# The opening of a hybrid block: raw rows into the projection, the root of the norm applied behind it, loads and first tables re-ordered

## The reference

```python
x = x + attn_a(ln(x))   # the "stack": Win 512 -> 64, 4 layers, Wout 64 -> 512
x = x + ffn(ln(x))      # gate, up, silu, down; weights w * (su @ sv), 512 -> 1792 -> 512
x = x + attn_b(ln(x))   # 32 heads, alibi, softmax, Wo
x = x + ffn(ln(x))      # the same weights again
# attn_a:
h = x @ Win.T + bin
for each of 4 layers:
    y = silu(layernorm(h) * ln1_w + ln1_b)
    h = h + sconv(y, phazor, last_conv) * sc_lin     # a complex linear recurrence over the sequence
    y = silu((layernorm(h) * ln2_w + ln2_b) @ W1.T + b1)
    h = h + y @ W2.T + b2
return (layernorm(h) * lnl_w + lnl_b) @ Wout.T + bout
```

## Time and profile before

| | |
|---|---|
| median of three runs | 2368.31 us |
| the profiled execution | 2372.38 us |
| its span in the trace | 2371.1 us |
| PE busy | 2328.1 us, 98% of the span |
| DVE, ACT, POOL busy | 67%, 51%, 35% |
| granted TensorE clock, mean | 0.993 of full speed |
| start of the first gate matmul | 117.28 us |

### The profile page before, as it was taken

How to read it: one execution, slowest core, us unless ns; L and a number is a source line. 1 busy time by engine, 2 the same in 40 slices (tenths; PEclk the granted TensorE clock), 3 DMA queues, 4 the chain that set the end, 5 groups by cost and what they waited for, 6 DMA issues and landing times.

```text
span 2371.1 us, 40814 instructions
## 1 busy us (share of the span) xinstructions
PE 2328.1 (98%) x12672; PEld 2015.7 (85%) x12672; DVE 1589.5 (67%) x3900; ACT 1218.3 (51%) x3827; POOL 838.5 (35%) x1332
## 2 busy tenths in 40 slices
PE   6899999999999999999999999999999999999999
PEld 4577777888899999999999999999999988888887
DVE  7666664534277777777777777777777776565553
ACT  7543332233266666666666666766766661232212
POOL 5550443212034445444454554444544440010000
PEclk8899999999999999999999999999999999999999
DMA  4335567987831534536346346364362225565554
GB/s 144 105 144 199 203 237 281 346 342 280 314 125 63 236 145 164 231 139 233 147 150 235 124 157 244 131 231 165 137 249 92 95 70 204 189 219 195 189 192 160
DMA packets 92627, 444.84 MB, mean 188 GB/s; under 512 B 10168, under 2 KB 17336, under 8 KB 72704
## 3 DMA queue, kind: packets, MB, share of 16 engines
q1 hardware_dynamic: 91056, 440.78, 50.5%
q10 hardware_dynamic: 1360, 1.46, 0.2%
HBM read 342.59 MB, written 99.61 MB: 186 GB/s over the span
## 4 chain that ended last, share of the span: by engine, by line
PE 93%; DVE 2%; DMA 1%; ACT 1%; POOL 1%; issue 1%; SPq 0%; DVEq 0%; POOLq 0%; ACTq 0%
PE psum L837 80%; PE psum L2832 4%; PE psum L2786 2%; PE psum L2821 1%; PE psum L2822 1%; PE psum L2777 1%; POOL x L1292 0%; POOL srstd L1262 0%; DMA wD<-weff_dn 0%; DMA short_raw<-in_lr_short 0%; DMA weff_s<-short_st 0%; PE psum L1812 0%; PE psum L1981 0%; PE psum L1959 0%; PE psum L1971 0%
## 5 line engine op out<-in xcount | busy, mean ns | idle before, releaser
L837 PE MATMUL psum<-qw,xs 128*128 128x384 f32 x2688 | 548.6, 346 | 0.2 <-DVE su L2630 0.2
L837 PEld LDWEIGHTS psum<-qw,xs 128*128 128x128 f32 x2688 | 457.8, 188 | 1.0 <-issue 0.4
L2603 POOL TENSOR_SCALAR prob<-prob,rsum 128x128 f32<-128x128 f32 (+1 forms) x512 | 228.9, 460 | 527.3 <-DVE rsum L2711 527.2
L2545 ACT ACTIVATE prob<-biased,nmax 128x256 f32<-128x256 f32 (+1 forms) x512 | 227.2, 446 | 151.0 <-DVE nmax L2701 147.7
L2719 DVE TENSOR_TENSOR oT_l<-psum,oT_h 128x512 fp32r<-128x512 f32 x128 | 88.5, 692 | 193.9 <-ACT oT_h L2557 193.9
L837 PE MATMUL psum<-wo_h,oT_h 128*128 128x512 f32 x512 | 208.5, 407 | 0.0
L837 PE MATMUL psum<-wo_l,oT_h 128*128 128x512 f32 x512 | 203.5, 397 | 0.0
L837 PE MATMUL psum<-wo_h,oT_l 128*128 128x512 f32 x512 | 202.0, 394 | 0.0
L2486 ACT ACTIVATE squares<-cc 128x128 f32<-128x128 f32 x512 | 154.3, 305 | 41.0 <-DVE cc L2633 31.4
L2552 ACT ACTIVATE pT_h<-psum 128x384 fp32r<-128x384 f32 x256 | 125.2, 489 | 76.1 <-PE psum L2832 73.7
L2569 POOL TENSOR_TENSOR rr<-ss,mneg_half 128x6 f32<-128x6 f32 (+1 forms) x128 | 150.1, 1173 | 10.7
(11 more groups left out here) (360 smaller groups left out, 5863.9 us busy)
## 6 DMA issues: line engine op xcount, KB each, us to landing
xs<-weff_x SPq DMA_DIRECT2D x62, 1792.0 KB, 7.9
wgu<-weff_gu SPq DMA_DIRECT2D x42, 1024.0 KB, 7.4
qw<-weff_q SPq DMA_DIRECT2D x56, 768.0 KB, 7.8
weff_q<-q_parts SPq DMA_DIRECT2D x84, 384.0 KB, 2.4
wD<-weff_dn SPq DMA_DIRECT2D x56, 512.0 KB, 4.8
wS<-weff_s SPq DMA_DIRECT2D x28, 1024.0 KB, 7.2
wdn<-weff_dn SPq DMA_DIRECT2D x42, 512.0 KB, 4.6
weff_gu<-wgu SPq DMA_DIRECT2D x14, 1024.0 KB, 4.0
```

Of the source, the lines that this page charges most:

```text
L837: ins = pe.matmul(out_ap, stat[a], mov[b], start=start and n == 0, stop=stop and n == last)
L2545: act.activation(prob[:, b, lo:hi], biased[:, b % 2, lo:hi], ACT.Exp, bias=nmax[:, b, t:t + 1], scale=-1.0, accum_out=esum[:, b, t:t + 1]) ...
L2603: pool.tensor_scalar(prob[:, b, lo:hi], prob[:, b, lo:hi], rsum[:, b, t:t + 1], 1.0, ALU.mult, ALU.mult).then_inc(prob_done, 1)
```

## The change

- **Rows.** The row step is gone. xT transposes the raw rows of x as soon as they have landed, and proj multiplies them. Win is centred over its input side too, so the mean of a row drops out: wcol (4 matmuls with a column of -0.5) gives the sums and one more DVE operation in winc subtracts them. The root of the norm is applied behind the projection: wide0 (ACT) copies the roots of four tiles out to 64 columns each, across (2 transposes) and roots (ACT copy) bring them along the columns, hs (DVE) multiplies. sq and h of norm 0 follow hs. This holds for all four stacks.
- **Odd norms of the lead.** w1 multiplies h itself, not the normed h. wc (two ACT copies of 128x512) takes the products out of PSUM; rtr makes the root for all 512 columns (four transposes), hm (two DVE products of 128x512) applies it, and hid works from SBUF. idw stands ahead of rtr. yn is gone here.
- **Norm 8, all stacks.** rtr, yn and wide are gone; out multiplies h, xadd multiplies by the root per row as it adds. The lead's second out waits for eps.
- **Products of the lead.** pr moves from DVE to POOL, pi from POOL to DVE.
- **Setting up.** root, rho, turn, tab0, scan0, winc and wcol get urgency 0. b1f now follows var 0.
- **Loads.** w1, b1, w2, wout and bout (seven DMAs, 1.3 MB) are issued by SP between the lead's rows and the rows of stack 1, instead of by ACT.
- **First gate.** Its first half takes the eight products with the high part of x and waits for fxhi alone; the second half, the four with the low part, waits for fxlo. frow 2 and 3 write into free buffers instead of the ring of two.

The diff, cut to its core (indentation shortened by eight; bookkeeping of semaphores and banks left out):

```diff
-    room = ("proj", 1, 0) if s == 3 else None
+    room = [("proj", 1, 0)] if s == 3 else []
...
-        o.add(("row", s, j), "dve" if lead else "act", 0.6, [("inv", 0, 2 * s + j // 2)] + ([("row", s, j - 1)] if j else [room] if room else []), urg,
-              ("row", 1))
-        o.add(("xT", s, j), "pe", 0.9 if lead else 0.45 * slow, [("row", s, j)] + ([("xc", s, j - 2)] if j > 1 and lead else []), urg,
-              bank, ("row", s, j))
-        step(("xc", s, j), "act", 0.6, [("xT", s, j)], ("xT", s, j))
-    pe_step(("proj", s, 0), 2.5 if lead else 1.75, [("xc", s, j) for j in range(TPB)] + [("winc", 0, 0)], bank)
+        landed = (("begin", 0, 0), 5.5 + 0.8 * j if lead else 13.0 + 3.0 * s)
+        o.add(("xT", s, j), "pe", 0.9 if lead else 0.45 * slow, [landed] + room + ([("xc", s, j - 2)] if j > 1 and lead else []) +
+              ([("xT", s, j - 1)] if j else [("xT", s - 1, TPB - 1)] if s else []), urg, bank)
+        step(("xc", s, j), "act", 0.6, [("xT", s, j)] + room, ("xT", s, j))
+    step(("wide0", s, 0), "act", 0.45, [("inv", 0, 2 * s), ("inv", 0, 2 * s + 1)])
+    pe_step(("across", s, 0), 0.25, [("wide0", s, 0), ("fold", 0, 0)], bank)
+    step(("roots", s, 0), "act", 0.4, [("across", s, 0)], ("across", s, 0))
+    pe_step(("proj", s, 0), 3.2 if lead else 1.75, [("xc", s, j) for j in range(TPB)] + [("winc", 0, 0)], bank)
+    step(("hs", s, 0), "dve", 0.43, [("proj", s, 0), ("roots", s, 0)], ("proj", s, 0))
...
-        made = ("conv", s, l) if odd else ("w2", s, l - 1) if n else ("proj", s, 0)
+        made = ("conv", s, l) if odd else ("w2", s, l - 1) if n else ("hs", s, 0)
...
-            step(("h", s, n), "dve", 0.42, [("sq", s, n)], made)
+            step(("h", s, n), "dve", 0.42, [("sq", s, n)], made if n else None)
...
+        if n == NORMS - 1:
+            break
+        if lead and odd:
+            pe_step(("w1", s, l), 1.5, [("h", s, n), ("fold", 2, l)])
+            pe_step(("idw", s, l), 0.45, [("h", s, n)])
+            step(("wc", s, l), "act", 1.3, [("w1", s, l)])
+            pe_step(("rtr", s, n), 0.45, [("rstd", s, n)])
+            step(("hm", s, l), "dve", 1.4, [("rtr", s, n), ("wc", s, l)])
+            step(("hid", s, l), "act", 1.3, [(("hm", s, l), -0.6), ("fold", 3, 0)])
+            pe_step(("w2", s, l), 0.9, [("hid", s, l), ("fold", 4, 0), ("idw", s, l)])
+            continue
...
-        if n == NORMS - 1:
-            break
...
-            step(("pi", s, l), "pool", 0.83, [("zi", s, l)])
-            step(("pr", s, l), "dve", 0.4, [("zr", s, l), ("zi", s, l)])
+            if lead:
+                step(("pr", s, l), "pool", 0.83, [("zr", s, l)])
+                step(("pi", s, l), "dve", 0.4, [("zi", s, l)])
+            else:
+                step(("pi", s, l), "pool", 0.83, [("zi", s, l)])
+                step(("pr", s, l), "dve", 0.4, [("zr", s, l), ("zi", s, l)])
...
-            if lead:
-                pe_step(("idw", s, l), 0.45, [("h", s, n)])
-            pe_step(("w2", s, l), 0.9, [("hid", s, l), ("fold", 4, 0)] + ([("idw", s, l)] if lead else []), bank)
+            pe_step(("w2", s, l), 0.9, [("hid", s, l), ("fold", 4, 0)], bank)
...
-        o.add(("bout", s, t), "pool", 1.27, [("fold", 5, 0), ("row", s, t), ("w1", 0, t) if lead else ("frow", 0, TPB - 1)], 6)
+        o.add(("bout", s, t), "pool", 1.27, [("fold", 5, 0), ("xT", s, t), ("inv", 0, 2 * s + t // 2), ("w1", 0, t) if lead else ("frow", 0, TPB - 1)], 6)
...
-        pe_step(("out", s, j), 0.95, [("yn", s, NORMS - 1), ("fold", 6, 0)], pair)
-        step(("xadd", s, j), "dve", 1.4, [("out", s, j), ("bout", s, j), ("bout", s, SJ + j)], ("out", s, j))
+        pe_step(("out", s, j), 0.95, [("h", s, NORMS - 1), ("eps" if lead else "rstd", s, NORMS - 1), ("fold", 6, 0)], pair)
+        step(("xadd", s, j), "dve", 1.4, [("out", s, j), ("rstd", s, NORMS - 1), ("bout", s, j), ("bout", s, SJ + j)],
+             ("out", s, j))
...
-    o.add(("root", 0, 0), "dve", 1.6, [("ri", 0, 0)], 1)
-    o.add(("rho", 0, 0), "act", 0.3, [("root", 0, 0)], 1)
+    o.add(("root", 0, 0), "dve", 1.6, [("ri", 0, 0)], 0)
+    o.add(("rho", 0, 0), "act", 0.3, [("root", 0, 0)], 0)
...
-        o.add(("turn", k, 0), "pool", 1.0 if k else 0.2, [("turn", k - 1, 0) if k else ("root", 0, 0)], 1)
-        o.add(("tab0", k, 0), "dve", 0.42 + 0.002 * (1 << k), [("turn", k, 0)] + ([("tab0", k - 1, 0)] if k else []), 1)
+        o.add(("turn", k, 0), "pool", 0.9 if k else 0.2, [("turn", k - 1, 0) if k else ("root", 0, 0)], 0)
+        o.add(("tab0", k, 0), "dve", 0.42 + 0.002 * (1 << k), [("turn", k, 0)] + ([("tab0", k - 1, 0)] if k else []), 0)
...
-    o.add(("winc", 0, 0), "dve", 1.0, [(began, 6.0)], 1)
-    o.add(("scan0", 0, 0), "dve", 1.2, [("root", 0, 0)], 1)
+    o.add(("wcol", 0, 0), "pe", 0.4, [(began, 4.8)], 0)
+    o.add(("winc", 0, 0), "dve", 1.6, [("wcol", 0, 0)], 0)
+    o.add(("scan0", 0, 0), "dve", 1.2, [("root", 0, 0)], 0)
...
-    o.add(("b1f", 0, 0), "pe", 3.6, [(began, 9.7)], 1, ("bank", 1, "early"))
+    o.add(("b1f", 0, 0), "pe", 2.2, [("var", 0, 0), (began, 9.7)], 1, ("bank", 1, "early"))
...
-            o.add(("gate", n, h), "pe", 1.36, here + [("fxlo", T, TPB - 1)] + ([last] if last else []) + (
+            o.add(("gate", n, h), "pe", 1.36 if n else (1.82, 0.91)[h], here + [
+                ("fxlo" if n or h else "fxhi", T, TPB - 1)] + ([last] if last else []) + (
...
+    for g in range(NG2):
+        rows = slice(g * DIM, (g + 1) * DIM)
+        sp.dma_start(w1_sb[rows, :, :], w1).then_inc(small_in, 16)
+    sp.dma_start(b1_sb[:], b1).then_inc(small_in, 16)
+    sp.dma_start(w2_c[:], w2).then_inc(w2_in, 16)
+    for g in range(NG2):
+        rows = slice(g * DIM, (g + 1) * DIM)
+        sp.dma_start(wout_sb[rows, :], wout).then_inc(wout_in, 16)
+    sp.dma_start(bout_sb[:], bout.partition_broadcast(P)).then_inc(wout_in, 16)
...
-    for g in range(NG2):
-        rows = slice(g * DIM, (g + 1) * DIM)
-        act.dma_start(w1_sb[rows, :, :], w1).then_inc(small_in, 16)
-    act.dma_start(b1_sb[:], b1).then_inc(small_in, 16)
-    act.dma_start(w2_c[:], w2).then_inc(w2_in, 16)
-    for g in range(NG2):
-        rows = slice(g * DIM, (g + 1) * DIM)
-        act.dma_start(wout_sb[rows, :], wout).then_inc(wout_in, 16)
-    act.dma_start(bout_sb[:], bout.partition_broadcast(P)).then_inc(wout_in, 16)
...
-        elif what == "row":
-            t = a * TPB + b
-            dst = wait_row(act, (what, a, b))
-            act.wait_ge(inv_done[0], 2 * a + b // 2 + 1)
-            act.activation(dst, x[:, t, :], ACT.Identity, bias=ln_nmr[:, t:t + 1],
-                           scale=ln_rstd[:, t:t + 1]).then_inc(stk_act[a], 1)
+        elif what == "wide0":
+            act.wait_ge(inv_done[0], 2 * a + 2)
+            roots = ln_rstd[:, a * TPB:(a + 1) * TPB].rearrange("p (g j o) -> p g j o", g=NG2, o=1)
+            act.activation(buf_b[q][:].rearrange("p (j g d) -> p g j d", j=SJ, g=NG2),
+                           roots.broadcast_to([P, NG2, SJ, DIM]), ACT.Copy).then_inc(stk_act[a], 1)
+        elif what == "roots":
+            act.wait_ge(stk_pe[a], ON_PE[a]["across", 0])
+            act.activation(buf_a[q][:], psum[:, stack_bank(a, "across", 0), 0:SW], ACT.Copy).then_inc(stk_act[a], 1)
...
+        elif what == "wc":
+            act.wait_ge(stk_pe[a], ON_PE[a]["w1", b])
+            bank = pair_bank(a, "w1", b)
+            for c in range(FC):
+                act.activation(hidden[:, q, c, :].rearrange("p (g t) -> p g t", g=NG2),
+                               psum[:, bank:bank + NG2, c * SW:(c + 1) * SW], ACT.Copy).then_inc(stk_act[a], 1)
...
-            act.wait_ge(stk_pe[a], ON_PE[a]["w1", b])
...
+            if lead:
+                for c in range(FC):
+                    act.wait_ge(stk_dve[a], ON_DVE[a]["hm", b, c])
+                    act.activation(hidden[:, q, c, :], hidden[:, q, c, :], ACT.Silu,
+                                   bias=b1_sb[:, b, c:c + 1]).then_inc(stk_act[a], 1)
+                continue
+            act.wait_ge(stk_pe[a], ON_PE[a]["w1", b])
...
-        elif what == "row":
-            dve_rows(wait_row(dve, (what, a, b)), 0, a * TPB + b).then_inc(stk_dve[a], 1)
+        elif what == "hs":
+            dve.wait_ge(stk_pe[a], ON_PE[a]["proj", 0])
+            dve.wait_ge(stk_act[a], ON_ACT[a]["roots", 0])
+            dve.tensor_tensor(hres[q][:], psum[:, stack_bank(a, "proj", 0), 0:SW], buf_a[q][:], ALU.mult).then_inc(stk_dve[a], 1)
...
-                ins = dve.tensor_scalar(hres[q][:], psum[:, stack_bank(a, "proj", 0), 0:SW], col_c("bin"), None, ALU.add)
+                ins = dve.tensor_scalar(hres[q][:], hres[q][:], col_c("bin"), None, ALU.add)
...
+        elif what == "pi":
+            dve.wait_ge(stk_dve[a], ON_DVE[a]["zi", b])
+            dve.tensor_tensor(buf_b[q][:], buf_a[q][:], sinT[:, b, :], ALU.mult).then_inc(stk_dve[a], 1)
+        elif what == "hm":
+            dve.wait_ge(stk_pe[a], ON_PE[a]["rtr", 2 * b + 1])
+            for c in range(FC):
```

(57 more changed lines are left out.)

72 lines of the change are left out of this document (45 added, 27 removed).

## The result

The changed kernel is slower: median 2375.78 us of 17 runs, against 2369.57 of as many runs of the kernel before; ratio 1.0023, 95% interval 1.0015 to 1.003. I had forecast 2363.1. Its profiled execution took 2377.15 us, its span is 2375.8, 4.7 above that of before.

The account below looks back on a forecast made before the run. TensorE was taken as full from 117.3 us, the lead's chain of waits as the bound before it. Terms +2.5 -0.5 -4.6 -4.0 -1.5 = -8.1, shadow +2.9, net -5.2: 2363.1 us, range 2354 to 2370.

Parts of the forecast that it names:

- Step 1: Opening up to silu: ACT stalls in lr 0 until its loads land near 20.4; +2.5 us.
- Step 2: Lead's even norms: pi on DVE ends sooner, pr on POOL hardly earlier; 0.15 us a layer, -0.5 us.
- Step 3: Lead's odd norms: shorter chain behind rtr, w1 and wc hidden; 1.15 us a layer, -4.6 us.
- Step 4: Norm 8: out no longer waits for the root, xadd applies it and ends earlier; -4.0 us.
- Step 5: First gate: starts right behind fxhi, its eight products hide fxlo, free frow buffers; -1.5 us.
- Shadow: TensorE work of other stacks that must run behind the earlier gate: 0.36 per us gained, +2.9 us.
- Sum: All five steps: -8.1 us at the first gate, near 109.2; net -5.2 us after shadow work is paid back.
- C: Opening, slower: 1.3 MB ahead in the queue delays low-rank loads to 26, lengthening ACT's stall; 2370.3 us; chance 0.1.
- B: Paid back: lead shortens, but shadow work falls behind and PE repays nearly all; -1.5, 2367 us; chance 0.2.
- A: Opening, no stall: lr 0 behind the lead's first steps or loads early; -17.6 at the gate, 2357 us; chance 0.2.
- The chance for slower: Whole kernel slower by over 0.2%: only the end of C and things not seen; chance 0.09.

Follow-up runs that it names:

- e6: Changed kernel with the eight small loads (w1, b1, w2, wout, bout) issued by ACT again, as before; median 2374.25 us.
- e1: Changed kernel with the swap undone: the lead's pr on DVE and pi on POOL again; median 2374.53 us.
- e18: Changed kernel with two planned times moved: lr 0 at 25.0, raw rows of stacks 1 to 3 at 22, 25, 28; median 2363.39 us.
- e11: Changed kernel with five spare 128x256 matmuls ahead of conv's wait for pr in each of the lead's layers 1 to 3; median 2369.40 us.
- e7: Kernel before the change with only norm 8 and the first gate changed; median 2367.77 us.
- e4: Changed kernel with five spare 128x256 matmuls ahead of the lead's wait for pr in all four layers; median 2372.45 us.
- e8: Kernel before the change with five spare 128x256 matmuls per lead layer ahead of conv's wait for pr; median 2379.45 us.
- e13: As e11, against the changed kernel, with the eight small loads also issued by ACT as before; median 2370.24 us.
- e17: e11 with lr 0 planned at 25.0 and raw rows of stacks 1 to 3 at 22, 25, 28; median 2365.48 us.
- e2: Changed kernel with one planned time moved: low-rank factors (lr 0) ready at 20.0 us instead of 12.0; median 2373.07 us.
- e16: e11 with lr 0 planned as ready at 20.0; median 2368.20 us.

## Why the prediction was wrong, step by step

**Step 1, right.** Forecast: lr 0 stalls ACT until 20.4, square at 25.4, silu at 30.7. Measured: 20.34, 25.50, 31.08; +2.9 on silu for +2.5. The order that I worked is the one that ran up to the first square. Between it and silu I was right by luck: I had two statistics there, 3.6 us, and the trace has one, with three copies of raw rows and a fold of wout in the other's place. The tables bound nothing, but they were ready at 28.33 and not near 21, because DVE stood in hs for 7.3 us and they were queued behind it. The table load was followed at once by silu, at 29.79 + 1.28 = 31.07 and 31.08, so the drain of 1380 ns of the Trainium skill (ScalarE: Activation LUTs, What ACT_TABLE_LOAD costs) is not seen here either. The first square is at 25.50 us with the loads issued by SP and at 25.44 with ACT (e6). By the rule of the Trainium skill (DMA: Bandwidth & Descriptors, Issuing engines are not separate DMA queues) moving issues saves issue time alone; this pair agrees, within the scatter of the landings given at e6.

**Step 2, near in size by luck, and blind to its effect.** The even blocks, from square to square, took 40.7 us for 41.55: -0.8 for -0.5 (-1.6 if layer 0 is counted from silu, as step 1 was). But the mechanism did not come. I had pi at 0.4 us on DVE and pr at 0.8 to 0.9 on POOL; they took 0.77 and 1.08 side by side, so the last operand was no earlier than before. pr's end was within 0.3 us of pi's, as I had written. The -1.6 is the sum of -0.1, -1.2, -1.8 and +1.6 us in the four layers, not of four times -0.15. And PE was left with 7.4 us of waits ahead of conv in three layers, where before there were 0.9. The swap is part of that: with it undone 3.6 us are left (e1), with the plan of e18 and the swap kept 3.7.

**Step 3, the step that failed.** Forecast -4.6, measured +1.0 (34.66 us for 33.64): 5.6 us of the 12.7, the largest piece. I had the mechanism: "at the lower clock TensorE's part doubles, w1 lasts 2.2 us", and put it into the range. I priced the step at full clock because norm 7 of before ran at full clock, without asking what kept it there. What ran instead is w1 at 2.08 us in three layers of four, with w1 and idw ahead of rtr, so that the root waited for them. e11 shows that the price was right for that clock (28.7 for 29.0).

**Step 4, right.** -4.65 for -4.0; alone, in e7, -3.8 on the additions.

**Step 5, failed.** Forecast -1.5, measured +0.8 (from the last addition to the gate 8.55 before, 9.31 after). The gate does start right behind fxhi, but eight transposes take 1.91 us twice instead of 1.07 and 1.08, which is 1.7 us. Ahead of them TensorE waits 2.70 us, a wait that before does not have. Every later kernel with the whole change or with the new odd norms has the half clock there in part or in full; e7, without those, does not (1.06 and 1.09), and gained 0.4 us.

**Shadow, failed.** Forecast +2.9, measured 6.25. At the clock of before it would have been about 6.25 - 5.3 = 1.0 for a gain of 1.55, near my 0.36 per us with the added work. e18 is the better test, with clock 1.00 behind its gate: of 12.5 us at the gate 3.4 are repaid by ACT's last gate copy (at 644.64) and 2.2 by the end, 0.27 and 0.18 per us. By its median, 6.2 to 8.5 us below before (2371.88 is the median of the before timed together with it), it is 0.3 to 0.5.

**Sum.** At the gate -1.55 instead of -8.1, so 6.55; behind it 3.35 more: together the 9.9 us between -5.2 and +4.7. In the steps' own terms the 6.55 are -0.3 (step 1, to the first square), -0.3 (step 2), +5.6 (step 3), -0.65 (step 4) and +2.3 (step 5). The other 2.8 of the 12.7 us on the median are the step from the profiled run to the median: I took off 4.1, the changed kernel's profiled run stood 1.4 above its median.

**Rivals.** C, the slower case, was the wrong mechanism: the loads landed at 20.34, not at 26. B (all paid back) foresaw the place and not the cause. A, no stall, has its experiment in e18: I had given -17.6 at the gate and 2357; it measured -12.5 and 2363.4, since wide0 waits for POOL's root until 16.60, and the square comes at 18.55, not 15.5; the rest is step 3 again (31.6 us, -2.1 for -4.6) and step 5. The chance for slower, 0.09, was too small because the one mechanism that I put there was chosen among the loads, while the mean clock of 0.85 ahead of the gate was taken as given, as if the change could not lower it.

**What stays open.** That the lower clock level comes with TensorE's waits in the lead is shown by e4 and e11 against after, with e8 as the control. Behind which single wait it comes isn't settled: the same 1.98 us behind the gate had it behind them in after, e13 and e17, and not in e2, e4, e6, e11, e16 and e18, and e18 kept a good time with 0.75 in one stretch. That e17 is slower than e18 because of the price of its spare matmuls is worked out, not shown by a run with fewer of them; its trace also has the lower level behind the gate (0.50 from 120 to 124 us), which e18's has not. And no run removes the 2.70 us ahead of the gate's transposes from the changed kernel, so step 5's part rests on the traces.

## What to carry to other kernels

When a change shortens the steps on other engines and leaves TensorE fewer matmuls between its waits, price each TensorE step at both clock levels (here w1 at 1.13 and 2.08 us), and check in the first profile whether its mean busy time per matmul has moved before looking for a cause elsewhere. Where a plan fixes the order, look at every planned landing time against the trace: in each in-order queue, the first instruction that waits for a late load holds everything behind it, and removing one such wait uncovers the next (ACT's lr 0, then TensorE's raw rows). And judge a small reordering by several neighbours of the kernel, not by one: here the same swap was worth -4.1 and +3.75 us.

## What the hardware showed that I had not expected

- Spare matmuls bought time: fifteen of 128x256, 0.46 us each, took 6.4 us off in e11; twenty cost 9.9 us in e8, where TensorE had no wait to fill.
- An idle time of 1.98 us (1.96 in e6) at the same place was followed by the lower level in three traces of nine: in e13, for one, 0.50 from 124 to 128, and not in e11.
- Two products of 128x256 side by side on POOL and DVE took 1.08 and 0.77 us, where alone in the same trace they took 0.73 and 0.42. So pi on the faster engine ended no earlier behind its scan than on POOL.
- The same loads, issued by the same engine in the same order, let lr 0 start at 20.34 in after and at 22.25 in e4.
